# Pixel statistics of a fused MetaFormer kernel: one bn_stats instruction for two pixels, interleaved through a strided read

## What is computed

```python
def _ln_c(v, eps=1e-6):                     # over the 96 channels of each pixel
    return (v - mean(v, axis=1)) / sqrt(var(v, axis=1) + eps)
def _ln_t(v, eps=1e-5):                     # the same on tokens (pixels as rows)
    return (v - mean(v, -1)) / sqrt(var(v, -1) + eps)
# layer 0
x = x + L0_conv(_ln_c(x))                   # 3x3 patches: cosine scores against 512 vectors, argmax,
                                            # mix, small MLP, 1x1 convolution back to a patch
t = tokens(x); t = t + ffn(_ln_t(t), W1, b1, W2, b2)      # 96 -> 384 -> 96 with 8-bit rounding
# layer 1
x = x + y / (2 + 1e-4 * box5x5(sum_c y*y)) ** 0.75        # y = _ln_c(x)
t = tokens(x); t = t + ffn(_ln_t(t), W1, b1, W2, b2)
```

## Time and profile before

| | |
|---|---|
| median of three runs | 3324.17 us |
| the profiled execution, its own time | 3325.16 us |
| its span, first to last instruction | 3323.4 us |
| granted TensorE clock, mean | 0.954 of full speed |
| busy: PE / DVE / ACT / POOL | 84% / 88% / 80% / 46% |
| DVE instructions | 10715 |

### The profile page before, as it was taken

One profiled execution on the slowest core, in us unless ns is written; L12 is line 12 of the kernel. 1 busy time (PEld: TensorE's weight loads), 2 busy tenths in 40 slices (PEclk: granted clock), 3 DMA queues, 4 the chain that ended last, 5 costly groups with the idle time before them and its releaser, 6 DMA issues.

```text
span 3323.4 us, 56026 instructions
## 1 busy us (share of the span) xinstructions
PE 2793.8 (84%) x15886; PEld 1506.5 (45%) x15886; DVE 2927.0 (88%) x10715; ACT 2646.0 (80%) x7047; POOL 1516.7 (46%) x1415
## 2 busy tenths in 40 slices
PE   5888988889899898888889898888888888888654
PEld 2444444444444454444445444444444445444322
DVE  6889999999999999999999999998998999989631
ACT  0444988989898888878888797888878788888877
POOL 1333444454445454544445454454544445445332
PEclk9999999999999999999999999999999999999755
DMA  3112232323232323223232323223233232232111
GB/s 92 49 57 57 66 77 69 85 69 85 69 85 69 85 69 85 70 74 78 68 85 75 79 75 80 69 78 73 69 84 68 68 85 69 73 78 59 37 45 48
DMA packets 236609, 237.33 MB, mean 71 GB/s; under 512 B 183427, under 2 KB 186765, under 8 KB 236301
## 3 DMA queue, kind: packets, MB, share of 16 engines
q1 hardware_dynamic: 226060, 214.86, 25.5%
q0 software_dynamic: 10240, 18.89, 2.1%
HBM read 134.72 MB, written 57.02 MB: 58 GB/s over the span
## 4 chain that ended last, share of the span: by engine, by line
PE 39%; ACT 21%; DVE 20%; DMA 13%; issue 5%; POOL 1%; SPq 0%; POOLq 0%; ACTq 0%; DVEq 0%
PE banks L416 13%; DMA ffn_xT<-ffn_x 12%; ACT ffn_hid L553 9%; PE banks L393 8%; ACT ffn_x L586 7%; PE banks L401 4%; DVE st L810 4%; ACT x L599 4%; PE banks L429 3%; DVE ffn_hid L898 3%; DVE pix L819 3%; PE banks L439 2%; PE banks L447 2%; PE banks L461 2%; DVE ffn_hid L906 2%
## 5 line engine op out<-in xcount | busy, mean ns | idle before, releaser
L553 ACT ACTIVATE ffn_hid<-banks 128x512 f16<-128x512 f32 (+1 forms) x2304 | 1065.6, 489 | 270.9 <-PE banks L393 237.3
L416 PE MATMUL banks<-wcT,xc 128*128 128x512 f32 x2304 | 1202.4, 612 | 51.1 <-DVE pix L819 33.3
L393 PE MATMUL banks<-ffn_xT,w1q 128*128 128x512 fp8e5 (+1 forms) x2304 | 727.1, 341 | 205.4 <-DMA ffn_xT<-ffn_x 109.0
L819 DVE TENSOR_REDUCE pix<-banks 128x1 f32<-128x512 f32 x1152 | 786.4, 683 | 36.5 <-PE banks L416 23.0
L401 PE MATMUL banks<-w2q,ffn_hid 128*128 128x96 bf16 x6912 | 400.3, 213 | 226.3 <-DVE ffn_hid L906 226.2
L1096 POOL TENSOR_TENSOR x<-x,ffn_f 128x864 f32<-128x864 f32 x256 | 483.6, 1889 | 209.3 <-DVE ffn_f L915 207.1
L393 PEld LDWEIGHTS banks<-ffn_xT,w1q 128*128 128x128 bf16 x2304 | 222.5, 98 | 756.6 <-ACT ffn_hid L553 447.3
L401 PEld LDWEIGHTS banks<-w2q,ffn_hid 128*128 128x128 f16 x6912 | 357.1, 102 | 377.6 <-issue 348.7
L416 PEld LDWEIGHTS banks<-wcT,xc 128*128 128x128 f32 x2304 | 408.4, 193 | 264.1 <-issue 191.8
L898 DVE TENSOR_SCALAR ffn_hid<-ffn_hid,b1q 128x1152 f16<-128x1152 f16 x768 | 411.5, 536 | 111.2 <-ACT ffn_hid L553 111.2
L599 ACT ACTIVATE x<-x,cols 128x96 f32<-128x96 f32 x1152 | 488.0, 459 | 19.1 <-POOL cols L1103 19.1
(11 more groups left out here) (139 smaller groups left out, 3267.5 us busy)
## 6 DMA issues: line engine op xcount, KB each, us to landing
xt<-x_tok_in SPq DMA_DIRECT2D x128, 432.0 KB, 4.3
xc<-x_chan_in SPq DMA_DIRECT2D x128, 432.0 KB, 5.4
out_tok<-x SPq DMA_DIRECT2D x128, 432.0 KB
ffn_xT<-ffn_x SPq DMA_TRANSPOSE x256, 2.9
win<-x_tok_in,xrow POOLq DMA_INDIRECT x128, 4.1
wrow<-vector_table,vidx POOLq DMA_INDIRECT x128, 2.7
shift<-shift_in SPq DMA_DIRECT2D x1, 960.0 KB
vector_table<-wtab SPq DMA_DIRECT2D x1, 384.0 KB, 2.9
```

Source lines behind the costliest of these rows:

```text
L393: last = pe.matmul(bank[:, 0:c1 - c0], w1q[:, ffn.layer, c * P:(c + 1) * P], pairs, start=True, stop=True)
L416: last = pe.matmul(ps_score[score_bank(j)], xc[p][:, j, :], wcT[:, :], start=True, stop=True)
L553: return nc.scalar.activation(dst, src, ACT.Copy)
L819: nc.vector.tensor_reduce(mx[p][:, j:j + 1], ps_score[score_bank(j)], AX.X, ALU.max).then_inc(score_taken, 1)
```

## The change

`bn_stats` now reads two pixels at once. The read goes through [128, 96, 2]: channel 0 of pixel a, channel 0 of pixel b, channel 1 of pixel a, and so on, with 96 elements (384 bytes) from one pixel to the other. So the even elements are the one pixel and the odd elements are the other, and the six numbers are finished statistics of two pixels. A group takes five instructions for nine pixels; the fifth reads pixel 8 twice (a stride of zero) and writes a tenth column that nobody reads. The numbers are written through a stride into `pix`, by kind: plane 0 counts, plane 1 means, plane 2 sums of squares, plane 3 the roots, each [4, 10]. `st3`, `mtmp` and five of the seven instructions of `moments` go; the wait on `kept` moves from `moments` to ahead of the statistics of `x2`. Readers of `twice` times -0.5 become readers of `mean` times -1, and L871 goes. The pieces of statistics become 2, 1, 2 (input), 2, 1, 2 (`x2`), 2 and 3 (`x1`) instructions.

```diff
@@ -165,17 +165,16 @@
         xt = sb("xt", [P, XT, J, C])
         xc = [sb(f"xc_{i}", [P, J, P]) for i in range(2)]
 
-        st3 = sb("st3", [P, 3, J, 6])
-
-        pix = [sb(f"pix_{i}", [P, 3, 4, J]) for i in range(2)]
-        twice = [b[:, 0, 0:3, :] for b in pix]
-        ssq = [b[:, 1, 0:3, :] for b in pix]
-        roots = [b[:, 2, :, :] for b in pix]
-
-        mx = [b[:, 1, 1, :] for b in pix]
-        mtmp = sb("mtmp", [P, 2, 3, J])
+
+
+        pix = [sb(f"pix_{i}", [P, 4, 4, 2 * PAIRS]) for i in range(2)]
+        mean = [b[:, 1, 0:3, 0:J] for b in pix]
+        ssq = [b[:, 2, 0:3, 0:J] for b in pix]
+        roots = [b[:, 3, :, 0:J] for b in pix]
+
+        mx = [b[:, 2, 1, 0:J] for b in pix]
         args = sb("args", [P, 4, J])
-        rtmp = sb("rtmp", [P, 4 * J])
+        rtmp = sb("rtmp", [P, 4, J])
         nb1 = sb("nb1", [P, J])
         sim = [sb(f"sim_{i}", [P, J]) for i in range(2)]
         top = [sb(f"top_{i}", [P, 8]) for i in range(2)]
@@ -207,7 +206,7 @@
 
 
         img = sb("img", [P, 3, SLOTS, J])
-        twice_i, ssq_i, rstd_i = (img[:, i, :, :].rearrange("p s j -> p (s j)") for i in range(3))
+        mean_i, ssq_i, rstd_i = (img[:, i, :, :].rearrange("p s j -> p (s j)") for i in range(3))
         r2_i, sq_i = sb("r2_i", [P, SLOTS * J]), sb("sq_i", [P, SLOTS * J])
 
         cols_i = sb("cols_i", [P, 4, SLOTS, J])
@@ -691,7 +690,8 @@
             nc.vector.memset(pow_half[:], -0.5)
             nc.vector.memset(eps[:, 0, :], 1e-5)
             nc.vector.memset(eps[:, 1:3, :], 1e-6)
-            nc.vector.memset(st3[:], 0.0)
+            for b in pix:
+                nc.vector.memset(b[:], 0.0)
             for c in chosen:
                 nc.vector.memset(c[:], 0.0)
 
@@ -765,49 +765,36 @@
                 if k.back is not None:
                     wait_past(dve, ffn0.x8_ready, k.back)
                 rc.begin(k.moments)
-                flat = lambda b: b.rearrange("p a j -> p (a j)")
-                y = flat(roots[k.p])
-                yield from inverse_root(rc, flat(args[:, :, :]), y, rtmp[:, :])
+                yield from inverse_root(rc, args[:, :, :], roots[k.p], rtmp[:, :, :])
                 rc.wait()
-                nc.vector.scalar_tensor_tensor(out=nb1[:, :], in0=twice[k.p][:, 0, :], scalar=-0.5,
+                nc.vector.scalar_tensor_tensor(out=nb1[:, :], in0=mean[k.p][:, 0, :], scalar=-1.0,
                                                in1=roots[k.p][:, 0, :], op0=ALU.mult,
                                                op1=ALU.mult).then_inc(root_ready, 1)
                 yield
 
-            MOMENTS = 7
+            MOMENTS = 2
             mc = Chain(dve, mom_chain, MOMENTS)
 
             def moments(tile, p):
-
 
                 dve.wait_ge(stats_ready, tile + 1)
                 wait_past(dve, root_ready, tile)
-                wait_past(dve, kept, tile - 6)
                 mc.begin(tile)
-                of = lambda i: st3[:, :, :, i]
-                d, m2 = mtmp[:, 0, :, :], mtmp[:, 1, :, :]
-                mc.add(nc.vector.tensor_tensor(d, of(1), of(4), ALU.subtract),
-                       nc.vector.tensor_tensor(m2, of(2), of(5), ALU.add))
-                yield
-                mc.wait()
-                mc.add(nc.vector.tensor_tensor(d, d, d, ALU.mult))
-                yield
-                mc.add(nc.vector.tensor_tensor(twice[p], of(1), of(4), ALU.add))
-                yield
-                mc.wait()
-                mc.add(nc.vector.scalar_tensor_tensor(out=ssq[p], in0=d, scalar=C / 4.0, in1=m2, op0=ALU.mult,
-                                                      op1=ALU.add))
-                yield
-                mc.wait()
                 mc.add(nc.vector.scalar_tensor_tensor(out=args[:, 0:3, :], in0=ssq[p], scalar=1.0 / C,
                                                       in1=eps[:, :, :], op0=ALU.mult, op1=ALU.add),
                        nc.vector.tensor_copy(args[:, 3, :], ssq[p][:, 1, :]))
                 assert mc.done == mc.per
                 yield
 
-            def group_stats(which, src, j0, j1, between):
-                for j in range(j0, j1):
-                    last = nc.vector.bn_stats(st3[:, which, j, :], src[:, j, :])
+            def group_stats(which, src, k, i0, i1, between):
+
+                if which == 2 and i0 == 0:
+                    wait_past(dve, kept, k.stats - 6)
+                for i in range(i0, i1):
+                    two = src[:, 2 * i:2 * i + 2, :] if 2 * i + 1 < J else src[:, J - 1:J, :].broadcast_to([P, 2, C])
+                    last = nc.vector.bn_stats(
+                        pix[k.q][:, 0:3, which, 2 * i:2 * i + 2].rearrange("p f t -> p t f"),
+                        two.rearrange("p t c -> p c t"))
                     run(between, 1)
                 return last
 
@@ -843,13 +830,13 @@
                 yield
                 f1c.wait()
                 one = pick[p][:, :].rearrange("p (o j) -> p o j", o=1).broadcast_to([P, 3, J])
-                f1c.add(nc.vector.tensor_tensor(junk[:, :, :], pix[p][:, :, 1, :], one, ALU.mult))
+                f1c.add(nc.vector.tensor_tensor(junk[:, :, :], pix[p][:, 1:4, 1, 0:J], one, ALU.mult))
                 yield
                 f1c.wait()
                 nc.vector.tensor_reduce(chosen[p][:, 0:3], junk[:, :, :], AX.X, ALU.add).then_inc(pick_ready, 1)
                 yield
 
-            f3c = Chain(dve, f3_chain, 6)
+            f3c = Chain(dve, f3_chain, 5)
 
             def win_vector(f2, q, between):
 
@@ -868,13 +855,12 @@
                 f3c.begin(f3)
                 f3c.add(nc.vector.tensor_reduce(dots[:, :], half_dot[:, :, :], AX.X, ALU.add),
                         nc.vector.tensor_scalar(mix[:, 0:1], chosen[q][:, 2:3], top_q, None, ALU.mult),
-                        nc.vector.tensor_scalar(mix[:, 2:3], chosen[q][:, 0:1], 0.5, None, ALU.mult),
                         nc.vector.tensor_scalar(mix[:, 1:2], top_q, -1.0, 1.0, ALU.mult, ALU.add))
                 meanwhile()
                 f3c.wait()
 
                 f3c.add(nc.vector.tensor_tensor(inp[:, C:C + J], dots[:, :], roots[q][:, 3, :], ALU.mult),
-                        nc.vector.tensor_scalar(wnorm[:, :], win[q][:, :], mix[:, 2:3], mix[:, 0:1],
+                        nc.vector.tensor_scalar(wnorm[:, :], win[q][:, :], chosen[q][:, 0:1], mix[:, 0:1],
                                                 ALU.subtract, ALU.mult))
                 f3c.wait()
                 run(between, 1)
@@ -940,7 +926,7 @@
                 yield
                 lc.wait()
                 lc.add(nc.vector.tensor_scalar(alpha, rg, 1.0, None, ALU.add),
-                       nc.vector.scalar_tensor_tensor(out=beta, in0=twice_i, scalar=-0.5, in1=rg,
+                       nc.vector.scalar_tensor_tensor(out=beta, in0=mean_i, scalar=-1.0, in1=rg,
                                                       op0=ALU.mult, op1=ALU.mult))
                 yield
                 lc.wait()
@@ -956,7 +942,7 @@
                 yield from inverse_root(lc, arg, rstd, t)
                 lc.wait()
                 assert lc.done == lc.per
-                nc.vector.scalar_tensor_tensor(out=bias, in0=twice_i, scalar=-0.5, in1=rstd, op0=ALU.mult,
+                nc.vector.scalar_tensor_tensor(out=bias, in0=mean_i, scalar=-1.0, in1=rstd, op0=ALU.mult,
                                                op1=ALU.mult).then_inc(lrn_ready, 1)
                 yield
 
@@ -980,15 +966,15 @@
                     if k.fs is not None:
                         if j0 == 0:
                             dve.wait_ge(xt_loaded[k.p], landed(k.fs, k.p))
-                        return group_stats(1, xt[:, k.fs & XT - 1], j0, j1, between)
+                        return group_stats(1, xt[:, k.fs & XT - 1], k, j0, j1, between)
                     return last
 
                 run(factors, 1)
                 scores(0, 1)
                 if k.f3 is not None:
-                    mlp_input(k.f3, k.p, roots_of, lambda: token_stats(0, 3))
+                    mlp_input(k.f3, k.p, roots_of, lambda: token_stats(0, 2))
                 else:
-                    token_stats(0, 3)
+                    token_stats(0, 2)
                 run(roots_of, 5)
                 scores(1, 2)
                 run(roots_of, 1)
@@ -998,32 +984,32 @@
                 run(factors, 1)
                 relu(ffn1, k.rear, 0)
                 scores(3, WIN_TURN, factors, 2)
-                last = token_stats(3, 6, factors)
+                last = token_stats(2, 3, factors)
                 if k.f2 is not None:
                     win_vector(k.f2, k.q, factors)
                 relu(ffn1, k.rear, 1)
                 scores(WIN_TURN, 5, factors, 2)
                 if k.tail is not None:
                     dve.wait_ge(x2_ready, k.tail + 1)
-                    group_stats(2, x2[:, k.tail & RING - 1], 0, 3, factors)
+                    group_stats(2, x2[:, k.tail & RING - 1], k, 0, 2, factors)
                 scores(5, 6, factors, 2)
```

(12 more changed lines are left out.)

## The result

The changed kernel takes 3360.0 us, median of five runs (3344.19 to 3366.39), against 3324.17 us (3317.73 to 3331.97). The ratio is 1.0093, interval 1.0068 to 1.0119: slower by 0.9%, which is some 31 us by the ratio (36 between the two medians), where 0.7% faster was forecast. DVE has less to do, as forecast; the time went elsewhere.

The account below looks back on a forecast made before the run. Two nearly equal routes, through DVE and through the transposing DMA, were taken to bound the kernel. 0.37 us by 62 steps gave 23 us, plus 4, less 3: 24 off, so 3300 us from 3324.2, range 3262 to 3440.

Parts of the forecast that it names:

- The price of a pair: Each paired `bn_stats` on DVE: 0.263 us of DVE time for 192 elements, replacing two that took 0.32.
- `moments`: Five DVE instructions removed, most of them free; 0.17 us less per step on the DVE route, bounds 0 and 0.55.
- the wait on `kept`: DVE's wait, moved ahead of the statistics of `x2`: POOL's copy is always past by then, so it costs nothing.
- Part 6: `lrn_columns` pieces in eight slots instead of fifteen: still end before `residual1`; nothing, at most 0.1 us every eighth step.
- The sum on the route: DVE route per step: 0.20 us from statistics plus 0.17 from `moments`, 0.37 us; by 62 steps, 23 us.
- the first rival: Transposing route also decides where the chain names DVE: nothing measurable, 3324 us, or 3316 with a third of the gain; chance 0.15.
- 62 decided steps: Steps the DVE route decides, from L906's 2% of the chain: 62 of 128, between 47 and 78 by rounding.
- the other route: Transposing route: PE's L393 of the second ffn, ACT, normalised pixels, DMA into `ffn_xT`, L393 again; nearly a step's length.
- the 22.4 us of the earlier trace: One passage of the transposing route, without DVE, from 947.60 to 969.99; the DMA takes 3.83 us of it.
- The rival that ended slower: Every strided pair instruction: hops between pixels cost further reads, DVE route grows; 3378 us mild, 3524 double; chance 0.23.
- a pair below 0.294 us: Break-even price of a pair instruction on the DVE route; above 0.294 us the route grows.

Follow-up runs that it names:

- e1: Changed kernel with all remaining pieces of `lrn_columns` issued ahead of `round_up` of the second ffn; 3324.15 us, ratio 0.9976 to the kernel before.
- e2: Kernel before, old statistics kept, with the last five pieces of `lrn_columns` falling behind `round_up`; 3368.56 us, ratio 1.012.
- e3: Changed kernel, DVE's order kept, but POOL waits for the last piece of `lrn_columns` before its products; 3335.27 us, ratio 1.0009.
- e5b: As e1, with three of fifteen pair instructions per step left out, their columns holding ones; 3318.86 us, ratio 0.997 to the kernel before.
- e7: As e1, with SP's load of `xc` issued behind the transposing DMA of the second ffn; 3214.79 us, ratio 0.9649 to the kernel before.
- e9: Kernel before, old statistics kept, with only SP's load of `xc` moved behind the transposing DMA; 3254.01 us, ratio 0.9776.
- e4: Changed kernel with each pair instruction reading its 192 elements side by side instead of alternating between pixels; 3354.07 us, ratio 1.0073 to the kernel before.
- e8: As e1, with nine pieces of `lrn_columns` between instructions of `inverse_root` and none behind `ffn_bias`; 3306.31 us, ratio 0.9913 to the kernel before.

## Why the prediction was wrong

**The price of a pair** held. Forecast 0.263 us of DVE's time and 350 ns; the timeline after shows three in 0.80 us, from 1509.10 to 1509.90:

```profile
1509.10 0.88 DVE L795 BATCH_NORM_STATS2 pix<-x 128x6 f32<-128x192 f32 x3
1509.90 0.67 DVE L806 TENSOR_REDUCE pix<-banks 128x1 f32<-128x512 f32 x1
1510.49 0.36 DVE L783 SCALAR_TENSOR_TENSOR args<-pix,eps 128x27 f32<-128x27 f32 x1
...
1510.84 0.16 DVE L816 TENSOR_TENSOR sim<-pix 128x9 f32<-128x9 f32 x1
1511.03 0.17 DVE L819 MAX8 top<-sim 128x8 f32<-128x9 f32 x1
...
1512.08 0.19 DVE L833 TENSOR_TENSOR junk<-pix,pick 128x27 f32<-128x27 f32 x1
1512.18 0.54 DVE L884 TENSOR_SCALAR ffn_hid<-ffn_hid,b1q 128x1152 f16<-128x1152 f16 x1
```

**`moments`** and the wait on `kept` went nearly as worked out: no wait of DVE for POOL's `img` appears. L829 to L832 of the earlier trace rows, now L816 (1510.84) to L819 (1511.03), is 0.19 us where 0.22 was forecast, and the `relu` starts 0.10 behind L833 (L846 of before), where 0.11 was forecast. L783 (`args`) takes the longer time that the first of the seven had.

**Part 6 failed, and it decided the result.** It said that the 21 pieces "still end before `residual1`; the last few go between the last statistics. Nothing, 0.1 us in every eighth step at most." The count was right and the price was wrong. Between the last statistics meant behind `round_up`, where POOL's products run; three pieces took 4.44 us there instead of 0.69, and the step grew by 4.35 in the mean, 61 us in 14 steps. The rows that showed the danger were in the profile of before and not among those I read for this part: there, L934 had a mean of 418 ns and L942 of 1980 for the same 72 elements that took L752 230 ns. L790 of `moments` itself, a two-input instruction of 27 elements, took 1.86 us in 14 steps beside a POOL instruction and 0.20 elsewhere. e1, e2 and e3 show the cause from three sides: the pieces moved, the old kernel with them late, and POOL held back.

**The sum on the route was too large.** Ordinary steps gained 0.04 us, not 0.37 in half of them. That is the first rival, that the transposing route holds everything, and I gave it 0.15. Reading 2% of the chain for L906 as 62 decided steps was too many: followed piece by piece, the chain of before passes whole through the `round_up` that ends a step in 47 steps, 14 of them with `lrn_columns` and 4 at the start, which leaves 29 ordinary ones. After the change it does so in 7 ordinary ones. So the other route stood close behind in most of them, as the 22.4 us of the earlier trace rows had suggested. The waits after, beside the earlier trace rows, show where DVE's saving went:

```profile
PE banks L400 <- DVE ffn_hid L892: 159.2, 138, 5.7
PE banks L392 <- DMA ffn_xT<-ffn_x: 152.6, 124, 3.8
...
DVE vidx L846 <- PE banks L428: 91.7, 116, 2.2
PE banks L415 <- DVE pix L806: 87.5, 22, 5.9
```

PE waits for L892 (L906 of before) 67 us less and for the transposing DMA 44 us more, and DVE waits for PE's L428 24 us more. e5b and e7 bear it out: less DVE work moved an ordinary step by 0.15 us, a lighter queue ahead of the transpose by 1.0. The 0.37 itself came out near where DVE holds more of the chain, 0.38 for e7 against e9. That is partly luck: it is a mean of 0.78 in one step of six and 0.30 in the others, DVE has 34 and 41% of these chains and not all, and the eight early steps gained 0.80.

**The rival that ended slower** had the wrong mechanism, a cost of the hop in every pair; e4 rules it out. That the kernel could get slower with a pair below 0.294 us was not among my cases at all.

**A side effect.** In the long steps PE waits longer for DVE; the last line of the waits has 22 waits of 4.0 us each, where the kernel before had 35 of 0.95. The granted clock of a step ahead, one with `lrn_columns` and one behind it (column PEclk, ahead of DMA share and GB/s):

```profile
1239.00:1265.00 26.00, 23.51 (x150) 14.25 (x149) 23.36 (x64) 20.16 (x54) 16.12 (x25) 1.00 0.28 71
1265.00:1297.50 32.50, 24.38 (x121) 12.69 (x120) 30.29 (x83) 20.56 (x56) 11.35 (x9) 0.84 0.22 57
1297.50:1321.80 24.30, 21.97 (x130) 12.14 (x131) 20.63 (x63) 22.45 (x62) 11.19 (x9) 1.00 0.31 76
```

It is 0.84 in the long step, a mean over 2.4 GHz and the lower level of 1.2, and full in the neighbours. It was 0.88 in the same step before; over the 14 long steps the mean is 0.94 before, 0.86 after and 0.91 in e1. The lower clock came with the longer waits and mostly went with them in e1, which fits an effect of the waits better than a cause of its own; how much of the 4.35 us it adds, no run here separates.

## What to carry to other kernels

When a change takes instructions away, ask what was threaded between them: the pieces of another chain slide later, and what matters is whom they then run beside. A DVE instruction with two SBUF inputs cost here its own time or that of the POOL product beside it, whichever ended later, so its place should be chosen by what POOL does then; a mean far above that of its size in the profile is the sign. And before paying for less work on the busiest engine, shorten the route that runs beside it: moving one load behind the transposing DMA was worth 2.2% on the old kernel, and only then did most of the saving on DVE show (1.3% between e9 and e7, 0.2% between the kernel before and e1).

## What was not expected of the hardware

- `bn_stats` alternating between two rows 384 bytes apart took 355 ns for 192 elements, against 351 side by side. The Trainium skill's exception for a single stream that alternates between two regions ("Vector Engine (DVE) Microarchitecture Reference", section 5.2) holds here, at a far smaller distance than its 16 KiB; its 1.73 ns a column for a hop at every element doesn't apply.
- A two-input DVE instruction of 72 elements stood still for the whole of a POOL product, 2.00 us instead of 0.23, and each further piece met the next product. Two kinds with one input were held too, a `TENSOR_SCALAR` (L939, 1976 ns in e8) and a copy (L785 after, 1844 ns in 14 steps against 158), while `bn_stats`, with one input as well, never was: of its 1920 in the changed kernel over a thousand began beside one of POOL's `TENSOR_TENSOR`, and none took more than 374 ns.
- Adding 1.06 us of DVE work to each step lengthened an ordinary one by 0.24 us, with DVE busy 85% of the span before it was added and 87% with it.
